# Moving waits about in a graph kernel with five engines near their limit: the last residual in two places, a new order of GpSimd's low parts, the last neighbour sums behind slot 1's gates, layer 1's rows loaded ahead of the sums

## The reference

```
def _layernorm(x, eps=1e-05):
    m = mean(x); v = var(x)
    return (x - m) / sqrt(v + eps)

# layer 0 (mean over weighted neighbours)
adj_norm = adj / (sum(adj, -1) + 1e-8)
h = relu(concat([x, adj_norm @ x]) @ weight + bias)
x = layernorm(x + h)

# layer 1 (gated graph network, 5 rounds l = 0..4)
A = (adj != 0)
h = x
for l in range(5):
    m   = h @ weight[l]
    agg = A^T @ m
    r = sigmoid(W_ir agg + W_hr h + b);  z = sigmoid(W_iz agg + W_hz h + b)
    n = tanh(W_in agg + b_in + r * (W_hn h + b_hn))
    h = (1 - z) * n + z * h
out = layernorm(x + h * mask)
```

## Time and profile before

| | |
|---|---|
| median of 3 runs | 622.47 us |
| profiled execution | 622.07 us, span 620.3 us |
| TensorE's granted clock, mean | 0.994 |
| busy, share of the span | PE 95%, DVE 89%, POOL 70%, ACT 64% |
| DMA queue of SP | 86.31 MB, 43% of 16 engines |

### The profile page before, as it was taken

One profiled execution on the slowest core, in us unless ns is written; L12 is line 12 of the kernel. 1 busy time (PEld: TensorE's weight loads), 2 busy tenths in 40 slices (PEclk: granted clock), 3 DMA queues, 4 the chain that ended last, 5 costly groups with the idle time before them and its releaser, 6 DMA issues.

```text
span 620.3 us, 9908 instructions
## 1 busy us (share of the span) xinstructions
PE 589.4 (95%) x2633; PEld 462.3 (75%) x2633; DVE 550.7 (89%) x1177; ACT 399.9 (64%) x764; POOL 435.5 (70%) x347
## 2 busy tenths in 40 slices
PE   7999999999999999999999999999999999999992
PEld 5677888777777777878777777877777777687772
DVE  5986979889999999999999999999999999877677
ACT  4867766767666585776757576675676668555551
POOL 0645554868789696887969687896887779675343
PEclk9999999999999999999999999999999999999997
DMA  7714114346363653736365373735537373210101
GB/s 257 296 35 132 38 36 158 114 151 223 101 228 93 216 156 106 246 116 227 101 202 170 101 239 107 234 114 171 190 109 237 104 221 118 86 51 2 51 1 51
DMA packets 92002, 86.66 MB, mean 140 GB/s; under 512 B 7760, under 2 KB 64080, under 8 KB 91984
## 3 DMA queue, kind: packets, MB, share of 16 engines
q1 hardware_dynamic: 91712, 86.31, 43.0%
q10 hardware_dynamic: 272, 0.13, 0.1%
HBM read 62.56 MB, written 23.86 MB: 139 GB/s over the span
## 4 chain that ended last, share of the span: by engine, by line
POOL 33%; PE 29%; issue 25%; DVE 7%; ACT 2%; DMA 2%; SPq 1%; POOLq 1%; DVEq 0%; ACTq 0%
POOL z_h L714 9%; POOL tok_lo L705 6%; POOL adjt_lo L641 5%; PE ps_tok L1501 4%; POOL tok_lo L698 3%; PE ps_tok L1494 2%; POOL h_lo L653 2%; POOL rstd L663 2%; PE ps_r L1336 2%; POOL cent L667 2%; POOL y_out L677 2%; PE ps_r L1338 2%; POOL rstd L647 2%; PE ps_r L1337 2%; PE ps_z L1338 2%
## 5 line engine op out<-in xcount | busy, mean ns | idle before, releaser
L714 POOL TENSOR_TENSOR z_h<-z_gate,h 128x512 f32<-128x512 f32 x80 | 105.5, 1319 | 19.4 <-ACT z_gate L921 18.9
L653 POOL TENSOR_TENSOR h_lo<-h,h_hi 128x512 fp32r<-128x512 f32 x64 | 84.6, 1322 | 47.2 <-ACT h_hi L741 47.2
L705 POOL TENSOR_TENSOR tok_lo<-rows,tok_hi 128x512 fp32r<-128x512 f32 x48 | 66.7, 1390 | 60.4 <-ACT tok_hi L741 60.3
L837 ACT ACTIVATE ps_in<-ps_in,gru_bias 128x512 f32<-128x512 f32 x80 | 53.0, 662 | 81.4 <-DVE ps_in L1191 81.0
L1501 PE MATMUL ps_tok<-edges,tok_lo 128*128 (+1 forms) x320 | 89.1, 400 | 5.0 <-POOL tok_lo L705 4.8
L1494 PE MATMUL ps_tok<-edges,tok_hi 128*128 (+1 forms) x320 | 88.2, 397 | 1.3 <-ACT tok_hi L741 1.3
L641 POOL TENSOR_TENSOR adjt_lo<-adjt_in,adjt_hi 128x512 fp32r<-128x512 f32 x56 | 77.4, 1404 | 2.3 <-ACT adjt_hi L741 2.3
L1501 PEld LDWEIGHTS ps_tok<-edges,tok_lo 128*128 128x128 f32 x320 | 58.8, 188 | 24.6 <-POOL tok_lo L705 11.3
L1494 PEld LDWEIGHTS ps_tok<-edges,tok_hi 128*128 128x128 f32 x320 | 59.4, 188 | 16.9 <-ACT tok_hi L741 2.1
L1229 DVE SCALAR_TENSOR_TENSOR ps_in<-z_gate,ps_in 128x512 f32<-128x512 f32 x80 | 55.6, 695 | 15.4 <-ACT ps_in L837 12.2
L1315 DVE SCALAR_TENSOR_TENSOR r_hn<-ps_hn,gru_bias,r_gate 128x512 f32<-128x512 f32 x80 | 58.9, 736 | 10.6 <-ACT r_gate L913 9.9
(11 more groups left out here) (177 smaller groups left out, 1575.3 us busy)
## 6 DMA issues: line engine op xcount, KB each, us to landing
adjt_in<-in_adj_t_dram SPq DMA_DIRECT2D x14, 1024.0 KB, 5.5
adj_in<-in_adj_dram SPq DMA_DIRECT2D x14, 1024.0 KB, 7.4
rows<-passage SPq DMA_DIRECT2D x192, 64.0 KB, 2.0
passage<-early_blocks SPq DMA_DIRECT2D x36, 256.0 KB, 2.0
x_in<-in_x_dram SPq DMA_DIRECT2D x16, 256.0 KB, 7.3
xt_in<-in_x_t_dram SPq DMA_DIRECT2D x15, 256.0 KB, 3.0
out_dram<-y_out SPq DMA_DIRECT2D x15, 256.0 KB, 2.3
passage<-last_blocks SPq DMA_DIRECT2D x14, 256.0 KB, 2.2
```

The costliest lines, as they stand in the source:

```text
L653: nc.gpsimd.tensor_tensor(h_lo[new][:], h[new][:], raw(h_hi[new][:]), ALU.subtract).then_inc(s_h_lo, 1)
L705: nc.gpsimd.tensor_tensor(tokens(tok_lo), rows_by_tokens(MOVED[slot + 1]), tokens(raw(tok_hi[:])), ALU.subtract).then_inc(s_tok_lo, 1)
L714: nc.gpsimd.tensor_tensor(z_h[:], z_gate[:], h[own][:], ALU.mult).then_inc(s_zh, 1)
```

## The change

- **DVE, last residual.** `pre2` is made in two places: pieces 0 to 2 in slot 1 where all four stood, piece 3 in slot 2 behind the new state's transposition, with its `bn_stats`. The `bn_stats` of 0 to 2 stay in slot 2. `bn_aggr` and `var2` go from ahead of slot 2's `r_hn` to behind it.
- **DVE, sums' blocks.** The transposition `late_blocks<-ps_b` goes from ahead of slot 1's `r_hn` to behind it.
- **PE.** Neighbour sums 2 and 3 go from ahead of slot 1's gate products to behind them.
- **SP.** The four loads of layer 1's rows stand ahead of the store of the neighbour sums.
- **POOL.** In slot 0 the order `adjt_lo(0)`, `adjt_lo(1)`, `tok_lo` becomes `adjt_lo(0)`, `tok_lo`, `adjt_lo(1)`. In slot 4 `h_lo[0]` goes ahead of `z_h`.
- **ACT.** In slot 4 `h_hi[0]` and `h[0]` go ahead of `z_gate`.
- The semaphore of the pieces is counted in two steps (`s_end_read`) for whoever waits for it.

```diff
@@ -572,11 +572,9 @@
                     store_state(w, 1)
+                    load_state(w, 1)
                 if w.means():
                     store_blocks(late_blocks, mean_passage, s_nsum_out, w.prepared(1, 1), s_mean_passed)
-                if w.trips():
-                    load_state(w, 1)
-                if w.means():
                     load_rows(mean_rows, mean_passage, s_mean_passed, w.passed(16, 1), s_mean_rows)
@@ -646,6 +644,12 @@
+                def moved_low(slot):
+
+                    pool.wait_ge(s_tok_hi, w.turned(slot + 2))
+                    nc.gpsimd.tensor_tensor(tokens(tok_lo), rows_by_tokens(MOVED[slot + 1]),
+                                            tokens(raw(tok_hi[:])), ALU.subtract).then_inc(s_tok_lo, 1)
+
                 def state_low(slot):
@@ -684,6 +688,8 @@
                             adjt_lo_of(0)
+                            if w.next_moved(slot):
+                                moved_low(slot)
                             adjt_lo_of(1)
@@ -699,25 +705,23 @@
                         last_norm()
-                    if w.next_moved(slot):
-
-                        pool.wait_ge(s_tok_hi, w.turned(slot + 2))
-                        nc.gpsimd.tensor_tensor(tokens(tok_lo), rows_by_tokens(MOVED[slot + 1]),
-                                                tokens(raw(tok_hi[:])), ALU.subtract).then_inc(s_tok_lo, 1)
+                    if w.next_moved(slot) and slot > 0:
+                        moved_low(slot)
                     if slot == 3 and w.first == 1:
...
                         state_low(slot)
-                    if w.unit(slot):
-
-                        pool.wait_ge(s_z, w.units(slot + 1))
-                        nc.gpsimd.tensor_tensor(z_h[:], z_gate[:], h[own][:], ALU.mult).then_inc(s_zh, 1)
                     if slot == 4 and w.means():
...
                                                 ALU.subtract).then_inc(s_h0_lo, 1)
+                    if w.unit(slot):
+
+                        pool.wait_ge(s_z, w.units(slot + 1))
+                        nc.gpsimd.tensor_tensor(z_h[:], z_gate[:], h[own][:], ALU.mult).then_inc(s_zh, 1)
+                    if slot == 4 and w.means():
                         state_low(slot)
@@ -913,16 +917,17 @@
                         x1_hi_of_batch()
+                    if slot == 4 and w.means():
+                        h0_parts_of_batch()
+                        evacuate(h[0][:], ps_b[1][:]).then_inc(s_h0, 1)
                     if w.unit(slot):
...
                         nc.scalar.activation(z_gate[:], ps_z[:], ACT.Sigmoid, bias=rz_bias[:, 1:2]).then_inc(s_z, 1)
-                    if slot == 4 and w.prepares():
+                    if slot == 4 and w.ramps():
                         h0_parts_of_batch()
-                    if slot == 4 and w.means():
-                        evacuate(h[0][:], ps_b[1][:]).then_inc(s_h0, 1)
                     if slot == 4 and (w.first == 1 or w.means()):
@@ -1132,7 +1137,7 @@
-                def pre2_of_batch():
+                def pre2_of(cs):
@@ -1143,7 +1148,7 @@
                     b = w.batch(3)
-                    for c in range(C):
+                    for c in cs:
                         last = nc.vector.scalar_tensor_tensor(
@@ -1202,8 +1207,9 @@
                             mean_parts(w)
-                        if slot == 2 and not w.ramps() and w.finishes():
-                            stats2_of_batch()
+                        if slot == 2 and w.finishes():
+                            dve.wait_ge(s_end_read, w.finished(2, 1))
+                            stats2_of((0, 1, 2))
                         if slot == 4 and w.leads():
@@ -1221,7 +1227,7 @@
                     if slot == 2 and w.idles():
-                        dve.wait_ge(s_end_read, w.finished(1, 1))
+                        dve.wait_ge(s_end_read, w.finished(2, 2))
                         stats2_of((0, 1, 2))
@@ -1234,7 +1240,8 @@
                     if slot == 1 and w.idles():
-                        pre2_of_batch()
+                        pre2_of((0, 1, 2))
+                        pre2_of((3,))
                     if slot == 4 and w.leads():
@@ -1260,13 +1267,17 @@
                     if slot == 1 and w.finishes() and not w.idles():
-                        pre2_of_batch()
+                        pre2_of((0, 1, 2))
+                        if not w.prepares():
+                            pre2_of((3,))
                         if slot == w.end_slot() and not w.prepares():
...
                     if w.finishes() and slot == 2 and w.prepares():
-                        moments2()
+                        pre2_of((3,))
+                        dve.wait_ge(s_end_read, w.finished(2, 2))
+                        stats2_of((3,))
                     if w.finishes() and slot == w.end_slot() and not w.idles() and not w.prepares():
@@ -1297,11 +1308,6 @@
                             nc.vector.reciprocal(row_inv[:], row_eps[:]).then_inc(s_rinv, 1)
-                            if w.means():
-                                dve.wait_ge(s_nsum, w.prepared(1, 1))
-                                nc.vector.transpose(late_blocks[:].rearrange("p q c j -> p c q j"),
-                                                    ps_b[2][:].rearrange("p (c q j) -> p c q j", c=C, q=Q)
-                                                    ).then_inc(s_nsum_out, 1)
                     if slot == 2 and w.first == 1:
@@ -1312,8 +1318,17 @@
                             dve.wait_ge(s_stats1, w.prepared(C, C))
+                        if slot == 2 and w.finishes() and w.prepares():
+                            dve.wait_ge(s_stats2, w.finished(C, C))
                         nc.vector.scalar_tensor_tensor(out=r_hn[:], in0=ps_hn[:], scalar=bhh_cols[:, 2:3],
                                                        in1=r_gate[:], op0=ALU.add, op1=ALU.mult).then_inc(s_rhn, 1)
+                        if slot == 1 and w.means():
+                            dve.wait_ge(s_nsum, w.prepared(1, 1))
+                            nc.vector.transpose(late_blocks[:].rearrange("p q c j -> p c q j"),
+                                                ps_b[2][:].rearrange("p (c q j) -> p c q j", c=C, q=Q)
+                                                ).then_inc(s_nsum_out, 1)
+                        if slot == 2 and w.finishes() and w.prepares():
+                            moments2()
                     if slot == 2 and w.first == 1:
@@ -1401,7 +1416,7 @@
                     if w.finishes():
-                        pe.wait_ge(s_end_read, w.finished(1, 1))
+                        pe.wait_ge(s_end_read, w.finished(2, 2))
                     for c in range(C):
@@ -1542,7 +1557,7 @@
                             own_products(1)
-                        if slot == 1:
+                        if slot == 1 and not w.means():
                             pe.wait_ge(s_own, w.prepared(2, 2))
@@ -1555,6 +1570,9 @@
                         gate(ps_in, 2, agg_hi, agg_lo, wi_hi, wi_lo, True, True).then_inc(s_in_sum, 1)
+                    if w.means() and slot == 1:
+                        pe.wait_ge(s_own, w.prepared(2, 2))
+                        neighbour_sums((2, 3), w.prepared(C, 0)).then_inc(s_nsum, 1)
                     if slot == 4 and w.ramps():
```

## The result

The kernel after takes **640.77 us** (median of 4 runs, 639.81 to 640.99), the kernel before 622.14 in the same comparison: ratio **1.029, 95% interval [1.0275, 1.0314]**. It is 18.6 us slower; 643 were predicted. The profiled execution after took 639.81 us, its span is 638.0.

The account below looks back on a forecast made before the run. DVE's queue plus its time blocked by POOL was taken to bound the loop. Terms 0.53 + 0.92 + 0.26 = 1.71 us per window, times 11, plus 1.6, gave 20.4 us on 622.47: 643 us, range 612 to 648.

Parts of the forecast that it names:

- The bound: Whole loop: in a long window DVE's queue plus its time blocked by POOL sets the length; PE's waits follow.
- Slot 1: DVE's sum with `r_hn` in slot 1 comes 0.53 us later per long window, as POOL's gap ahead of `tok_lo` closes.
- Slot 2: DVE's sum with `r_hn` in slot 2 comes 0.92 us later per long window, as `var` waits for POOL's `z_h`.
- Slot 4 and 0: Turn to slot 0: `xt_lo` waits for `h_lo[0]`, `z_h` for `xt_lo`; new state and slot 0 come 0.26 us later.
- The sum: Whole kernel: 1.71 us lost per long window, over 11 windows, plus 1.6 for the short ones: 20.4 us, giving 643 us.
- The two short windows: Two of 12 windows, 35.90 us each, lose 0.8 us more, as the late load behind POOL's idling now delays nothing.
- PE's waits for `agg_lo` in slots 2 and 3: Sign of a right forecast, on PE in slots 2 and 3: these waits would be over 1 us each.
- The rival in which PE gets what was meant for it: Slot 1's gap survives and PE's waits go: 14 us faster, 608 us, or 615 if half comes; chance 0.24.

Follow-up runs that it names:

- e2: Kernel after, with one wait added: in slot 1 POOL starts `tok_lo` only when DVE's `row_eps` is done; 611.28 us, ratio 0.984.
- e3: Kernel after, with `var` of the last norm (4 columns, slot 2) made on ACT instead of DVE; 631.92 us, ratio 1.018.
- e8: Kernel after, with slot 1's `row_eps` addition on ACT instead of DVE, the reciprocal staying on DVE; 626.47 us, ratio 1.010.
- e1: Kernel after, with POOL's order in slot 0 as before (both `adjt_lo`, then `tok_lo`); 626.08 us, ratio 1.009.
- e5: Kernel after, with PE's neighbour sums 2 and 3 back ahead of slot 1's gates; 629.13 us, ratio 1.015.
- e4: Kernel before, with only POOL's `tok_lo` of slot 0 moved between the two `adjt_lo`; 620.16 us, ratio 1.000.
- e9: Kernel before, with only PE's neighbour sums 2 and 3 moved behind slot 1's gates; 627.94 us, ratio 1.011.
- e6: Kernel after, with the order of slot 4 on ACT and POOL as before; 633.08 us, ratio 1.022.

## Why the prediction was right

**The bound.** Right. DVE's queue with its blocked time sets the window: e2, e3 and e8 shorten only stalls, and the windows get shorter by 2.9, 0.85 and 1.34 us.

**Slot 1, predicted 0.53 later, measured 0.61** (5.33 - 4.72). The order was exact: pieces at P, at the end of `tok_lo` and of `h_lo`, `row_eps` at the end of `z_h`. Both causes named are shown: PE's punctuality closes the gap ahead of `tok_lo` (e1 opens it again, 1.0 to 1.5 us per window), and the earlier `z_gate` closes that ahead of `z_h` (e5, 1.1 us). The prediction told them as two facts in a row; e4 shows that the first costs nothing while the second gap is open, and e9 that the second alone costs 1.1 us in most windows. What it didn't see, as it read a single window: in six of the nine long windows before, the third piece was held as well, and the gap ahead of `z_h` made up for it (the lines are under e9). Its P + 4.72 was right all the same, since both ways end there.

**Slot 2, predicted 0.92, measured 0.77.** `var` was caught by `z_h` for 0.97 us; e3 gives back 0.85 per window. `z_h` came when predicted (a + 3.37 to a + 4.66); the term is too large because the sum with `r_hn` starts 0.09 ahead of `var`'s recorded end (248.53 and 248.62), not 0.1 behind it.

**Slot 4 and 0, predicted 0.26; e6 measures 0.30.** `xt_lo` and `z_h` pay for each other as told (0.99 and 1.75 us), but the new state comes only 0.16 later by it. The other half comes in slot 0, where `edges` and what stands beside it take 0.15 longer (under e6); the prediction didn't name that. That the sizes agree is partly luck.

**The sum.** 0.61 + 0.77 + 0.30 = 1.68 for 1.71, by windows 38.32 - 36.72 = 1.60. The two short windows of before went as well, as counted. The predicted 643 is 2.2 us above the 640.8 measured: ten windows carry the loss and not eleven, and the errors of the three terms (0.08 too small, 0.15 too large, 0.04 too small) nearly cancel.

**What was wrong.** PE's waits for `agg_lo` in slots 2 and 3 were to be over 1 us each; they are 0.84 and 0.54. The largest wait of PE, 1.4 to 1.5 us for `r_hn` ahead of slot 2's state products, wasn't named; it is the same late DVE, met earlier. The rival in which PE gets what was meant for it is real but not by this change: a wait on POOL brings it (e2, 611.3, where 608 to 615 were worked out).

**What stays open.** The transposition behind `r_hn`, the fourth piece's place in slot 2 and SP's earlier loads were never turned back by themselves. With the loads ahead, slot 2's `tok_lo` starts at a + 0.47 instead of a + 1.74, and `z_h` with it comes early enough to catch `var`; how much of slot 2's loss is the loads' and how much the new place of `var` isn't shown.

## What to carry over

When an engine's instructions are held by another's, look for the idle gaps in the other's queue before removing a wait: those gaps may be what lets the first one through, and a punctual engine can close them. Count what passes in each gap, in every window and not in one: two windows of the same length can come about in different ways, and the second way is what hides how narrow the first gap is. A kernel that depends on some 20 ns is better given its gap by an explicit wait, or relieved of the held instructions (tiny ones above all, which cost as much as long ones) by an engine that isn't held. An edit that measures as nothing alone, as e4 does, may only have used up a reserve.
